# Moving one tile's weighted sum ahead of the next tile's gathers on GpSimd

## The chip, the cores and the metric

One core of one Trainium2 chip. The metric is device microseconds of one execution. Each kernel runs several times; the median is quoted with its lowest and highest run. A separate profiled execution gives the trace, and all times "at" a moment are microseconds from the start of its span.

## The reference, cut to what matters

Input is x of shape (4, 512, 128): four sequences of 512 rows, 2048 rows in all. Four layers follow, each wrapped in a residual and a layer normalisation:

```python
x = _layernorm(x + _L0_attn_ref(x, ...))   # state-space mixer
x = _layernorm(x + _L0_ffn_ref(x, ...))    # mixture of experts: 64 experts, top 8 for each row, and a shared one
x = _layernorm(x + _L1_attn_ref(x, ...))   # attention, 16 heads of 8 columns, bias terms, no mask
x = _layernorm(x + _L1_ffn_ref(x, ...))    # three dense layers with weights of +1 and -1
...
# of the experts' layer:
rw = zeros(T, E).at[rows, topk_idx].add(topk_w)        # 8 weights for each row
routed = jnp.einsum('eth,te->th', expert_out, rw)      # each row's 8 weighted expert rows, summed
out = routed + shared
```

The change concerns the place between the second and the third layer: the weighted sum of each row's 8 expert rows, the normalisation behind it, and the attention that needs it.

## The kernel before, in words

The 2048 rows are 16 tiles of 128 rows (`NT = 16`), four tiles to a sequence (`TB = 4`). Each engine has its own instruction stream, written out by hand, and the streams meet at semaphores.

**Experts.** Rows are scattered to blocks by expert in DRAM (`xd`), pairs of blocks go through the expert's matmuls, and results are written to DRAM (`od`). The first half (tiles 1 to 7) and the second half (tiles 8 to 15) have arrays of their own. For each tile the 8 result rows of each row are then gathered back by 8 indirect DMAs that GpSimd issues (`bring`, L533). For the later tiles GpSimd also forms the sum (`sum_rows`): one multiplication with the weights (L545), three halving additions (L547), one addition of the shared part that writes `tmp` (L548). Each step waits for the one before it, and then `summed` is raised.

**Normalisation.** VectorE waits for `summed`, takes statistics of the four tiles of a sequence (L845, L848) and raises `s_st`. GpSimd makes the reciprocal root from them (`rstd_of`, L469 and L470) and raises `s_rstd`. VectorE then writes the normalised rows (L856), TensorE transposes them (L1516), and ScalarE and TensorE make queries and keys from them.

**Attention.** 16 groups, four for each sequence (`NGR = 16`, `GB = 4`). In group i TensorE does the scores of group i (L1577), their products with the values (L1587) and ahead of time the scores of group i + 2 for the row maxima (L1567). VectorE takes those maxima (L1136), splits them at the end of each group (L1164 to L1173) and normalises the output of the group before (L1150, L1154). ScalarE does the exponentials (L748). The later sequences are prepared inside the groups of the one before: the tables `LATER` and `STATS_IN` set the places. For sequence 2 (tiles 8 to 11) VectorE takes statistics at the end of group 3, and normalisation and transposes stand in group 4. For sequence 3 (tiles 12 to 15) the statistics stand at the end of group 7, the rest in group 8. Sequence 2 is split into parts by VectorE (L1092 to L1098), sequence 3 by GpSimd.

In `dve_group`, the wait that stands between the end of group 3 or 7 and the next group:

```python
if isinstance(i, int) and i + 1 in STATS_IN:
    v.wait_ge(summed, TB * (STATS_IN[i + 1] + 1) - MINE - DENSE)
    stats(tmp, STATS_IN[i + 1])
```

**GpSimd's stream around the change.** While the groups run, GpSimd works through the second half: the 8 gathers of tile t, then the sum of tile t - 1, for t = 9 to 15, and last the sum of tile 15. The root of sequence 2, `rstd_of(2 * B + 2)`, stands behind the first two gathers of tile 13. The root of sequence 3 stands behind the sum of tile 15. Tile t's rows land in a slot of their own (`back_slot`); the slots are four, so tile 12 uses tile 8's slot.

Of the kernel before, what the change touches and what calls it, by code (L numbers as in the profile page):

```python
# [25 lines left out]
TOP_K = 8  # L26
# [5 lines left out]
def build(nc, x, a_log, dmat, w_in, b_in, w_xp, b_xp, w_out, b_out, gamma, beta,  # L32
# [5 lines left out]
    TB = L // P  # L38
# [40 lines left out]
    SLOTS = ((1, 2), (2, 2), (3, 0))  # L79
    STATS_IN = {4: 2, 8: 3}  # L80
    TURN_IN = {i: b for (i, _), (what, b) in LATER.items() if what == "x"}
    PARTS_AT = ((0, 2, 1), (0, 3, 0), (0, 3, 1), (0, 3, 1), (1, 0, 0), (1, 0, 1))
    WRITE_IN = {2: 1, 6: 2, 10: 3}
# [37 lines left out]
    with ExitStack() as ctx:  # L121
# [127 lines left out]
        def back_slot(t):  # L249

            n = t - FIRST[1]
            if n < 0:
                return gb[:, t % 4]
            return late_slot if n % 4 == 3 else gb2[:, n % 4]
# [200 lines left out]
        def _(pool):  # L455
            pn = [0]

            def own(ins):

                pn[0] += 1  # L460
                ins.then_inc(s_p, 1)
                pool.wait_ge(s_p, pn[0])

            def rstd_of(k):

                pool.wait_ge(s_st, k + 1)
                q = k % B
                r = rstd[:, TB * q:TB * q + TB]
                own(pool.tensor_scalar(r, mv[:, TB * q:TB * q + TB, 1], EPS, None, ALU.add))  # L469
                pool.tensor_tensor(r, r, minus_half[:], ALU.pow).then_inc(s_rstd, 1)  # L470
# [57 lines left out]
            def bring(f, t, slot, first=0, last=TOP_K):  # L528

                for k in range(first, last):  # L530
                    if t > DENSE:
                        pool.wait_ge(g_in[k], 16 * (t - DENSE))
                    pool.indirect_dma_start(out=slot[:, k], out_offset=None, in_=od[f],  # L533
                                            in_offset=bass.IndirectOffsetOnAxis(ap=idx[:, t, k:k + 1], axis=0)).then_inc(g_in[k], 16)

            def landed(t):
                for k in range(TOP_K):
                    pool.wait_ge(g_in[k], 16 * (t - DENSE + 1))

            def sum_rows(t):  # L540

                landed(t)
                pool.wait_ge(s_wk, 4 * (t + 1))
                slot = back_slot(t)
                own(pool.tensor_tensor(slot, slot, wk[:, t].unsqueeze(2).broadcast_to([P, TOP_K, M]), ALU.mult))  # L545
                for n in (4, 2, 1):
                    own(pool.tensor_tensor(slot[:, 0:n], slot[:, 0:n], slot[:, n:2 * n], ALU.add))  # L547
                own(pool.tensor_tensor(tmp[:, t], slot[:, 0], xb[:, t], ALU.add))  # L548
                pool.sem_inc(summed, 1)
# [19 lines left out]
            bring(1, FIRST[1], back_slot(FIRST[1]))  # L569
            rstd_of(2 * B + 1)  # L570
            for t in range(FIRST[1] + 1, NT):
                bring(1, t, back_slot(t), 0, 2)
                if t == 3 * TB + 1:
                    rstd_of(2 * B + 2)
                bring(1, t, back_slot(t), 2, TOP_K)
                sum_rows(t - 1)
            sum_rows(NT - 1)

            def qk_parts(b):
# [746 lines left out]
        def _(pe):  # L1326
# [158 lines left out]
            def pe_pairs(first, s0, pairs, beside=None, copied=None, last=None):  # L1485

                ids = {}

                def load_ids(quad, quads=1):

                    _, got = nc.values_load_multi_w_load_instructions(
                        tab[0:1, bass.ds(first + (AHEAD + 4 * quad), 4 * quads)], engines=[mybir.EngineType.PE],
                        min_val=0, max_val=E - 1, skip_runtime_bounds_check_because="the table holds minima with E - 1")
                    for n in range(4 * quads):
                        ids[4 * quad + n] = got[n]

                load_ids(-3, 3)
                for u in range(pairs):
                    later = pairs == 8 and u in (1, 3, 5)
                    pe_pair(s0 + u, u, lambda b: ids[b], (lambda: load_ids(u // 2)) if later else None, beside, copied)  # L1500
                    if last is not None:
                        last(s0 + u)
# [314 lines left out]
```

## Time and profile before

| what | before |
|---|---|
| median of 3 runs | 670.5 us (669.43 to 671.48) |
| the profiled execution: its time, its span | 670.14 us, 668.4 us |
| busy share: TensorE matmul, VectorE, ScalarE, GpSimd | 89%, 72%, 59%, 56% |
| mean granted TensorE clock | 0.953 |
| chain that ended last, by engine | TensorE 57%, VectorE 12%, GpSimd 10%, DMA 7% |
| GpSimd's gathers L533 | 120 of them, about 1 us each |

The busy shares are means over stages with different limits. The row of the chain says which engine's work stood last in line: TensorE most of the time, with stretches of GpSimd in between. The granted clock is 1.00 or 0.50 in any one moment (2.4 or 1.2 GHz); a mean of 0.953 says that it was at the lower level for a few stretches.

### The profile page before, as it was taken

To read this page: it belongs to the slowest core of one execution; us is meant where nothing else is said; L and a number is where in the kernel's file an instruction comes from. 1 tells how busy PE (TensorE), PEld (TensorE's weight loads), DVE (VectorE), ACT (ScalarE), POOL (GpSimd) and SP (SyncE) were. 2 spreads that over 40 slices of the span, in tenths; PEclk is the share of its full clock that TensorE was granted. 3 is DMA by queue.
4 is the path that set the end of the run, shared out by engine and by line. 5 is a ranking of instruction groups with operands and counts; after the bars stand their busy time and mean duration, and the time that the engine had idled before them with its cause. 6 is when DMAs were issued, how large, how long until landed. Compare 5 with 4: busy or idle time off the path is not lost.

```text
span 668.4 us, 13071 instructions
## 1 busy us (share of the span) xinstructions
PE 594.4 (89%) x3696; PEld 371.4 (56%) x3697; DVE 480.3 (72%) x1226; ACT 395.3 (59%) x896; POOL 372.0 (56%) x398
## 2 busy tenths in 40 slices
PE   3973999879999999999886999799989999888994
PEld 2252666659999999999761333233323234344552
DVE  5469743555556656778679788788878886869886
ACT  3411454326666666667657877467777778866541
POOL 6321777777777217775707787887746000235652
PEclk9976799989999999999986999899999999999998
DMA  5999951136777668887454254125203200000001
GB/s 173 434 370 221 399 184 52 52 126 193 225 221 223 197 173 226 224 219 196 131 180 112 70 158 107 42 89 146 53 31 107 71 2 2 1 0 1 17 17 31
DMA packets 98998, 91.51 MB, mean 137 GB/s; under 512 B 10707, under 2 KB 84531, under 8 KB 98739
## 3 DMA queue, kind: packets, MB, share of 16 engines
q1 hardware_dynamic: 91275, 75.24, 37.0%
q0 software_dynamic: 7680, 15.74, 8.3%
q8 instruction: 21, 0.34, 0.2%
q14 instruction: 22, 0.18, 0.1%
HBM read 44.87 MB, written 45.61 MB: 135 GB/s over the span
## 4 chain that ended last, share of the span: by engine, by line
PE 57%; DVE 12%; POOL 10%; DMA 7%; issue 5%; SPq 4%; ACT 3%; POOLq 0%; DVEq 0%; ACTq 0%
PE ps L1472 11%; PE ps L1459 8%; PE ps L1587 6%; PE ps L1577 6%; DMA arena<-zeros 6%; POOL arena L533 4%; PE ps L1567 4%; PE ps L1467 4%; PE ps L1482 4%; PE ps L1384 3%; PE ps L1389 3%; SPq L348 2%; DVE mx L1136 2%; DVE arena L1254 2%; DVE arena L1246 1%
## 5 line engine op out<-in xcount | busy, mean ns | idle before, releaser
L1136 DVE TENSOR_REDUCE mx<-ps 128x2 f32<-128x1024 f32 x128 | 150.9, 1218 | 29.2 <-PE ps L1567 28.6
L748 ACT ACTIVATE big<-ps 128x512 f32<-128x512 f32 x256 | 141.1, 597 | 41.3 <-PE ps L1577 38.6
L521 POOL DMA_INDIRECT xd<-xt,idx x120 | 120.1, 1001 | 49.4 <-issue 35.6
L1472 PE MATMUL ps<-arena,xbT 128*128 x496 | 97.2, 319 | 4.0 <-DVE xbT L1062 4.0
L533 POOL DMA_INDIRECT big<-od,idx x72 | 71.4, 992 | 49.4 <-DMA od<-big 25.0
L1577 PE MATMUL ps<-arena 128*128 128x512 bf16 (+1 forms) x256 | 85.9, 388 | 5.6 <-ACT big L748 4.5
L1058 DVE TENSOR_TENSOR hm<-sg,ps 128x176 f32<-128x176 f32 x124 | 41.8, 337 | 67.0 <-ACT sg L687 65.4
L1567 PE MATMUL ps<-arena 125*128 125x512 bf16 (+1 forms) x256 | 71.8, 394 | 9.2 <-DVE mx L1136 9.0
L1472 PEld LDWEIGHTS ps<-arena,xbT 128*128 128x128 f32 x496 | 76.2, 194 | 4.9 <-issue 4.8
L1459 PE MATMUL ps<-arena,hmT 96*128 x496 | 77.4, 279 | 1.1 <-ACT hmT L683 1.1
L677 ACT ACTIVATE big<-ps 128x256 f32<-128x256 f32 x124 | 47.7, 384 | 47.8 <-PE ps L1459 47.6
L1587 PE MATMUL ps<-big,keep 128*32 128x512 f32 x512 | 69.0, 611 | 0.0
L1577 PEld LDWEIGHTS ps<-arena 128*128 128x128 bf16 (+1 forms) x256 | 20.7, 97 | 86.0 <-ACT big L748 42.9
L1459 PEld LDWEIGHTS ps<-arena,hmT 96*128 96x128 f32 x496 | 65.6, 192 | 3.8 <-issue 1.9
L533 POOL DMA_INDIRECT arena<-od,idx x48 | 46.7, 973 | 32.4 <-DMA od<-big 16.3
L469 POOL TENSOR_SCALAR rstd<-mv 128x4 f32<-128x4 f32 x20 | 5.4, 270 | 102.0 <-DVE mv L848 101.9
L1649 PE MATMUL ps<-arena 128*128 128x512 bf16 x240 | 54.1, 379 | 2.3 <-DVE arena L1246 2.3
L687 ACT ACTIVATE sg<-ps 128x176 f32<-128x176 f32 x124 | 39.4, 318 | 28.0 <-PE ps L1472 23.7
L1062 DVE COPY xbT<-ps 128x256 f32<-128x256 f32 x124 | 51.8, 418 | 0.0
L1467 PE MATMUL ps<-idf,hm 128*96 128x128 f32 x248 | 48.1, 275 | 2.4 <-DVE hm L1058 2.4
L1482 PE MATMUL ps<-idf,big 128*128 128x128 f32 x248 | 48.3, 277 | 0.7 <-DVE xb L912 0.4
L1567 PEld LDWEIGHTS ps<-arena 125*128 125x128 bf16 (+1 forms) x256 | 23.2, 98 | 46.0 <-DVE mx L1136 21.6
(219 smaller groups left out, 994.3 us busy)
## 6 DMA issues: line engine op xcount, KB each, us to landing
big<-xd SPq DMA_DIRECT2D x62, 256.0 KB
od<-big SPq DMA_DIRECT2D x62, 256.0 KB
arena<-scr SPq DMA_DIRECT2D x96, 96.0 KB
xd<-zeros SPq DMA_DIRECT2D x1, 8192.0 KB, 60.5
xd<-zeros SPq DMA_DIRECT2D x1, 7680.0 KB, 21.9
arena<-w_gu SPq DMA_DIRECT2D x1, 5632.0 KB
scr<-places SPq DMA_DIRECT2D x8, 384.0 KB, 2.8
arena<-w_d SPq DMA_DIRECT2D x1, 2560.0 KB
```

The source lines that it names most:

```text
L521: pool.indirect_dma_start(out=xd[f], out_offset=bass.IndirectOffsetOnAxis(ap=idx[:, t, k:k + 1], axis=0), in_=xt[:, t], in_offset=None).th ...
L533: pool.indirect_dma_start(out=slot[:, k], out_offset=None, in_=od[f], in_offset=bass.IndirectOffsetOnAxis(ap=idx[:, t, k:k + 1], axis=0)). ...
L748: act.activation(ering[:, HG * (mt % 2) + h], ps[:, 4 + h % 2, :], ACT.Exp, scale=SCALE).then_inc(exp_ready, 1)
L1136: v.tensor_reduce(mx[:, k, TB * h + 2 * a:TB * h + 2 * a + 2], ps[:, 2 * a:2 * a + 2, :], AX_X, ALU.max).then_inc(s1_free, 1)
L1459: ins = pe.matmul(ps[:, 6 + (u - DN) % 2, M * a:M * a + M], hmT[0:KI, (u - DN) % 2, a], wd_s[0:KI, bass.ds(expert(2 * (u - DN) + a), 1), : ...
L1467: ins = pe.transpose(ps[0:KI, 4 + (u - TH) % 2, P * a:P * a + P], hm[:, (u - TH) % 2, a], idf[:])
L1472: ins = pe.matmul(ps[:, 2 + (u - GU) % 2, I2 * a:I2 * a + I2], xbT[:, (u - GU) % 2, a], wgu_s[:, bass.ds(expert(2 * (u - GU) + a), 1), :]. ...
L1482: ins = pe.transpose(ps[:, u % 2, P * a:P * a + P], xin[:, quad, 2 * part + a], idf[:])
L1567: ins = pe.matmul(ps[:, c, :], flat(kst[0:KM, head(i, h), P * c:P * c + P]), flat(qst[0:KM, head(i, h), :]), start=True, stop=True)
L1577: pe.matmul(ps[:, 4 + h % 2, :], flat(qst[:, head(i, h), P * mt:P * mt + P]), flat(kst[:, head(i, h), :]), start=True, stop=True).then_inc ...
L1587: ins = pe.matmul(ps[32 * h:32 * h + 32, 6, :], vs[:, k, mt, h], ering[:, HG * (mt % 2) + h], start=(mt == 0), stop=(mt == TB - 1))
L1649: ins = pe.matmul(ps[:, n % FC, :], w, h1[b % 2][:, part, kk] if layer else xp[:, part, L * b:L * b + L], start=(kk == 0 and part == 0), s ...
```

## The change

Tile 11's sum now stands in front of tile 12's gathers. The root of sequence 2 stands behind the fourth gather of tile 12, where it stood behind the second gather of tile 13. Elsewhere the order of the loop is as it was.

```diff
             for t in range(FIRST[1] + 1, NT):
-                bring(1, t, back_slot(t), 0, 2)
-                if t == 3 * TB + 1:
+                if t == 3 * TB:
+                    sum_rows(t - 1)
+                bring(1, t, back_slot(t), 0, 4)
+                if t == 3 * TB:
                     rstd_of(2 * B + 2)
-                bring(1, t, back_slot(t), 2, TOP_K)
-                sum_rows(t - 1)
+                bring(1, t, back_slot(t), 4, TOP_K)
+                if t != 3 * TB:
+                    sum_rows(t - 1)
             sum_rows(NT - 1)
```

GpSimd's stream around tile 12, as a difference. The first rows are the end of tile 10's sum; the sum that reads `big` is tile 11's, in whose slot its gathers landed; `rstd` is the root of sequence 2; the `L533` rows are the gathers:

```order
 L547 TENSOR_TENSOR arena<-arena 128x128
 L548 TENSOR_TENSOR tmp<-arena,xb 128x128
-L533 DMA arena<-od,idx 128x128 x8
 L545 TENSOR_TENSOR big<-big,wk 128x1024
 L547 TENSOR_TENSOR big<-big 128x512
```

The eight gathers of tile 12 no longer stand between the sums of tiles 10 and 11. The same stream further on, from the end of tile 11's sum to the beginning of tile 12's:

```order
 L547 TENSOR_TENSOR big<-big 128x128
 L548 TENSOR_TENSOR tmp<-big,xb 128x128
-L533 DMA arena<-od,idx 128x128 x2
+L533 DMA arena<-od,idx 128x128 x4
 L469 TENSOR_SCALAR rstd<-mv 128x4
 L470 TENSOR_TENSOR rstd<-rstd,minus_half 128x4
-L533 DMA arena<-od,idx 128x128 x6
+L533 DMA arena<-od,idx 128x128 x12
 L545 TENSOR_TENSOR arena<-arena,wk 128x1024
```

Four gathers of tile 12 stand ahead of the root, and behind it the other four and the eight of tile 13. The streams of the other engines and of the DMA queue on SyncE have the same instructions in the same order.

## Rows read from the trace of the kernel before

**Rows 1.** The chain of waits: start, length in us, what stood last.
```profile
429.25 1.05 POOL rstd L470
430.34 1.34 DVE xt L856 x4
```

**Rows 2.** Timeline of GpSimd, tiles 11 to 13: start, us, engine, line, operation, idle before.
```profile
404.00 0.94 POOL L533 DMA_INDIRECT big<-od,idx  x1 [0.30 <-issue]
...
409.64 0.45 POOL L548 TENSOR_TENSOR tmp<-arena,xb 128x128 f32<-128x128 f32 x1
410.90 0.98 POOL L533 DMA_INDIRECT arena<-od,idx  x1 [0.81 <-POOL tmp L548]
...
420.65 1.92 POOL L545 TENSOR_TENSOR big<-big,wk 128x1024 f32<-128x1024 f32 x1
...
425.39 0.46 POOL L548 TENSOR_TENSOR tmp<-big,xb 128x128 f32<-128x128 f32 x1
...
429.25 1.04 POOL L470 TENSOR_TENSOR rstd<-rstd,minus_half 128x4 f32<-128x4 f32 x1
430.49 1.16 POOL L533 DMA_INDIRECT arena<-od,idx  x1 [0.19 <-DMA arena<-od,idx]
```

**Rows 3.** Timeline of VectorE, end of group 3 and start of group 4.
```profile
421.56 1.04 DVE L1164 SCALAR_TENSOR_TENSOR mp<-mx,zeros 128x16 bf16<-128x16 f32 x1
...
423.01 0.96 DVE L1170 CAST mp<-mr 128x16 bf16<-128x16 f32 x1
...
425.93 0.87 DVE L845 BATCH_NORM_STATS2 st<-tmp 128x6 f32<-128x128 f32 x4 [1.75 <-POOLq L549]
```

**Rows 4.** Timeline of VectorE, end of group 7.
```profile
482.54 0.17 DVE L1164 SCALAR_TENSOR_TENSOR mp<-mx,zeros 128x16 bf16<-128x16 f32 x1
...
483.42 0.86 DVE L845 BATCH_NORM_STATS2 st<-tmp 128x6 f32<-128x128 f32 x4
```

**Rows 5.** Timeline of GpSimd, tile 15's sum and the root of sequence 3.
```profile
477.55 1.90 POOL L545 TENSOR_TENSOR big<-big,wk 128x1024 f32<-128x1024 f32 x1 [0.53 <-POOL tmp L548]
479.53 2.61 POOL L547 TENSOR_TENSOR big<-big 128x512 f32<-128x512 f32 x3
482.22 0.45 POOL L548 TENSOR_TENSOR tmp<-big,xb 128x128 f32<-128x128 f32 x1
484.79 0.23 POOL L469 TENSOR_SCALAR rstd<-mv 128x4 f32<-128x4 f32 x1 [2.12 <-DVE mv L848]
485.11 1.04 POOL L470 TENSOR_TENSOR rstd<-rstd,minus_half 128x4 f32<-128x4 f32 x1
```

**Rows 6.** Timeline of TensorE's matmuls, start of group 4.
```profile
428.38 0.89 PE L1567 MATMUL ps<-arena 125*128 125x512 bf16 x2 [2.16 <-DVE mx L1136]
...
431.81 1.09 PE L1516 MATMUL ps<-idf,xt 128*128 128x128 f32 x4 [1.27 <-DVE xt L856]
...
435.50 0.60 PE L1577 MATMUL ps<-arena 128*128 128x512 bf16 x2
```

**Rows 7.** The same, start of group 8.
```profile
488.23 0.63 PE L1516 MATMUL ps<-idf,xt 128*128 128x128 f32 x4 [0.63 <-DVE xt L856]
...
490.21 0.69 PE L1577 MATMUL ps<-arena 128*128 128x512 bf16 x2
```

**Rows 8.** Stretches: length, TensorE's busy time, granted clock, DMA share, GB/s.
```profile
357.00:367.00 10.00, 7.14 (x15) 0.50 0.39 107
...
428.00:429.00 1.00, 0.62 (x2) 0.79 0.22 66
429.00:435.00 6.00, 4.49 (x17) 0.50 0.17 44
435.00:436.00 1.00, 1.00 (x7) 0.80 0.10 25
```

**Rows 9.** Timeline of GpSimd: tile 12's halving additions, the second gather of tile 15.
```profile
439.92 3.24 POOL L547 TENSOR_TENSOR arena<-arena 128x512 f32<-128x512 f32 x3
...
463.43 0.95 POOL L533 DMA_INDIRECT big<-od,idx  x1 [2.07 <-issue]
```

## The prediction

> **What bounds the kernel now.** I read the chain of waits first, then the timelines of GpSimd, VectorE and TensorE around the place that the chain names, and last the same stretch one sequence later. The attention groups run at TensorE's pace, and twice the chain leaves TensorE for the stage that prepares the next sequence. The first meeting is at the end of group 3. In the chain there, the root of sequence 2 on GpSimd (L470) releases VectorE's normalisation (L856), which releases TensorE's transposes (L1516) [rows 1]. On GpSimd tile 10's sum ends at 409.64 + 0.45 = 410.09. Tile 12's eight gathers follow from 410.90, though tile 11's last gather was issued at 404.00. Only at 420.65 does tile 11's sum begin, and it ends at 425.39 + 0.46 = 425.85 [rows 2]. VectorE came to the statistics of tiles 8 to 11 earlier: it sat idle 1.75 us before 425.93, so since 424.18, and it would have come sooner still, for L1164 and L1170 took 1.04 and 0.96 us while the sum's long operations ran [rows 3]. At the second meeting, at the end of group 7, VectorE needs tile 15's sum. Its L1164 starts at 482.54 and the statistics at 483.42 with no idle time [rows 4]. GpSimd finished tile 15 at 482.22 + 0.45 = 482.67 [rows 5], 0.75 us before. That is the number on which this prediction turns: GpSimd has 0.75 us to spare there and no more.
>
> **The change at the first meeting.** Nothing is added or removed; eight gathers move behind one sum, and the root behind four gathers of tile 12 instead of two of tile 13.
>
> Tile 11's sum can start at once behind tile 10's. Two sums in a row are 0.53 us apart [rows 5], so it starts at 410.09 + 0.53 = 410.62, runs 425.85 - 420.65 = 5.20, and ends at 415.82 instead of 425.85. Its data are there: the last gather was issued 6.6 us earlier, and a gather's whole pitch is 0.94 + 0.30, about 1.25 us [rows 2].
>
> VectorE at the end of group 3 is then alone. From L1164 to the statistics took 424.18 - 421.56 = 2.62 us [rows 3], and 0.88 at the end of group 7, where no sum ran beside it [rows 4]. So the statistics start at 421.56 + 0.88 = 422.44 instead of 425.93. The root follows as at the second meeting, where L469 starts 1.37 us after the statistics and L470 ends 1.36 us after that [rows 4, 5]: L469 at 423.81, root done 425.17, where it was 430.29.
>
> TensorE's transposes stood at 488.23 in group 8, 4.81 us behind the statistics, and at 431.81 in group 4, 5.88 behind them [rows 6, 7]. So they move to 422.44 + 4.81 = 427.25, a gain of 4.56 us. After them TensorE needed 3.69 us in group 4 to its second pair of L1577 (435.50), but 1.98 in group 8 (490.21) [rows 6, 7], because the granted clock in group 4 was 0.50, the lower of its two levels, after it had sat idle until 428.38 and again before 431.81; in the stretch before 435 it was still 0.50 [rows 8]. With the shorter wait I take group 8's pace, which adds 3.69 - 1.98 = 1.71. **First term: -4.56 - 1.71 = -6.27 us**, and VectorE would reach the second meeting at 483.42 - 6.27 = 477.15.
>
> **The change at the second meeting.** GpSimd does not share this gain, because the same change gives it a wait. Tile 12's gathers start 0.81 us behind the sum as they did before (410.09 to 410.90), so at 415.82 + 0.81 = 416.63. Four of them at the pitch of 1.25 end at about 421.3, with the first a little longer. Then comes the root, and it needs VectorE's statistics, ready for it only at 423.81: GpSimd stands for 2.5 us. Queued behind that wait are four gathers of tile 12, all of tiles 13 to 15, and the sums of 12 to 15, which is everything that the second meeting waits for.
>
> The end of tile 15's sum: before, the root ended at 430.29, and from there to 482.67 GpSimd needed 52.38 us for 6 gathers of tile 13, the 16 of tiles 14 and 15 and four sums. After the root there are now six gathers more (4 of tile 12 and 8 of tile 13, against 6), 6 x 1.25 = 7.5. So 425.17 + 52.38 + 7.5 = 485.05. The statistics of tiles 12 to 15 start at 485.13 with the 0.08 us seen at the first meeting (425.85 to 425.93), instead of 483.42. **Second term: +1.71 us instead of -6.27.** All that groups 4 to 7 gain becomes idle time of VectorE, 477.15 to 485.13, 8 us.
>
> TensorE drains behind it and stands for about as long, longer than at the first meeting before. There the clock fell. So group 8 now pays what group 4 paid, and group 4's saving is already spent. **Third term, the clock: +1.71 us**, by the same pair of rows. Its lower bound is nothing, if the clock is back before the transposes. Its upper bound is from the stretch 357 to 367, where the clock stayed at 0.50 for 10 us with TensorE busy 7.14 of them [rows 8]; half of that work is 3.6 us. I take 1.71, since that stall is the nearest in kind: same engines, same instructions. The Trainium skill (TensorE: Matmul & The Clock Gate, "HAM oscillation — how this bites in real kernels") charges half of the whole time at the lower clock. By that rule the 6.8 us of group 4 (0.4 of the slice from 428, the 6 to 435 and 0.4 of the next) [rows 8] would cost 3.4, and the sum would be +5.1. The trace shows only 1.71 for them, as part of that time was waiting anyway.
>
> Small items. Groups 4 to 7 meet GpSimd's sums at other moments, which may hold VectorE's short operations again; those have 8 us of cover. GpSimd can be held too: tile 12's three L547 took 3.24 us beside VectorE's splitting of sequence 2, against 2.61 for tile 15's [rows 5, 9]. I leave that 0.6 as it is, with 0.6 either way for the range. A gap of 2.07 us stands before a gather of tile 15 [rows 9]; what it waits for is not shown, and it is counted as it stands. The other engines' orders do not change, and from group 9 on everything follows at the same distance.
>
> **Sum:** +1.71 + 1.71 = +3.4 us on a span of 668.4 us, so 671.8, and 670.1 + 3.4 = 673.5 for that execution. Against the median of the runs, 670.5, which stands 0.4 above it, the forecast is **673.9 us**. About 0.3%, or 2.0 us, is what a measurement of this kernel can tell from no change.
>
> **The rivals.**
> - *The low clock lasts long.* A wait of 8 us is longer than any shown at these meetings, and TensorE could stay at the lower level for the 10 us of 357 to 367: 1.71 + 3.6 = +5.3, so 675.8. For it speaks the length of the stall; against it, that TensorE is fully busy soon after the transposes, which it was not there.
> - *The clock costs nothing more.* Only the second term is left, +1.7: 672.2, which is no measurable change. Against it is the fall after a much shorter stall [rows 8].
> - *The gap closes on GpSimd.* If the 2.07 us gap before the gather of tile 15 vanishes with the new timing, tile 15's sum ends at 482.98, and the second term is -0.4. With the clock's 1.7 that is +1.3, 671.8: no measurable change.
> - *The gain stays.* Place: VectorE's wait at the end of group 7. If tile 15's sum were done when VectorE arrives at 477.15, no second stall would come, and the full first term would remain: 664.2. It decides at an end of tile 15's sum of about 481.6, where the second term would just pay the clock (483.42 - 1.71 - 0.08). Some of the gain stays below that. Against it: GpSimd is serial and had no pause near 7 us between 410 and 482; its issue gaps of 0.30 belong to each gather. An unseen faster pitch with fewer holds would have to save over 3.4 us.
> That the change does not do what it says can be set aside: the order shows it, and tile 11's gathers were issued long before.
>
> **How the numbers follow.** Forecast 0.55, long low clock 0.15, no clock cost 0.12, the gap closes 0.12, the gain stays 0.06. Slower by over 0.3%: the forecast and the long clock, 0.70. Within 0.3%: the two in the middle, 0.24. Faster: 0.06. The range leaves out the gain that stays and the ends of the others. It reaches down to the closed gap, 671.8 less 0.6 of contention, 671.2; and up to the long clock plus 0.6 and 0.4 of scatter, 676.8.
>
> **What would show each step.** Tile 11's sum at 410.6 and the root done near 425.2; L1164 and L1170 at the end of group 3 back at 0.2 us; GpSimd idle 2.5 us before L469 behind four gathers; the transposes of group 4 near 427.3 with no fall of the clock there; the sum of tile 15 ending near 485; VectorE idle 7 to 8 us before the statistics of tiles 12 to 15; the clock at 0.50 in group 8 instead of group 4. I am wrong if GpSimd ends tile 15 before 483, if VectorE's wait is not there, or if the clock stays up through it.

## The result and the profile after

| | before | after |
|---|---|---|
| median, runs | 670.36 us, 7 (669.24 to 671.48) | 674.99 us, 7 (672.50 to 676.20) |
| ratio | | 1.0063, 95% interval 1.0046 to 1.0080 |
| profiled execution: time, span | 670.14, 668.4 us | 673.07, 671.3 us |
| mean granted TensorE clock | 0.953 | 0.956 |

The kernel became slower, by 4.2 us as a ratio of 670.36 us. In the two profiled executions the span grew by 2.9 us. The runs after fall into two kinds: three at 672.5, 673.0 and 673.1 us and four from 675.0 to 676.2. The profiled one is of the first kind.

The execution after stood 0.34 us ahead of the one before when the change began (tile 10's sum ends at 409.75 instead of 410.09), so a moment after is compared with the moment before less 0.34. The line numbers from L572 on are higher by 3.

GpSimd's timeline around tiles 11 and 12 (start, us, engine, line, operation, idle before), which answers to [rows 2]:

```profile
410.27 1.90 POOL L545 TENSOR_TENSOR big<-big,wk 128x1024 f32<-128x1024 f32 x1 [0.53 <-POOL tmp L548]
...
414.94 0.45 POOL L548 TENSOR_TENSOR tmp<-big,xb 128x128 f32<-128x128 f32 x1
416.20 0.98 POOL L533 DMA_INDIRECT arena<-od,idx  x1 [0.81 <-POOL tmp L548]
...
419.99 0.94 POOL L533 DMA_INDIRECT arena<-od,idx  x1 [0.30 <-issue]
423.41 0.23 POOL L469 TENSOR_SCALAR rstd<-mv 128x4 f32<-128x4 f32 x1 [2.48 <-DVE mv L851]
423.73 1.04 POOL L470 TENSOR_TENSOR rstd<-rstd,minus_half 128x4 f32<-128x4 f32 x1
```

Tile 11's sum starts at once behind tile 10's. The four gathers follow, and then GpSimd stands for 2.48 us, until VectorE's aggregates (L851) are there. The root ends at 424.77; before it was 430.29.

VectorE at the end of group 3, against [rows 3]:

```profile
421.16 0.17 DVE L1167 SCALAR_TENSOR_TENSOR mp<-mx,zeros 128x16 bf16<-128x16 f32 x1
...
422.04 0.87 DVE L848 BATCH_NORM_STATS2 st<-tmp 128x6 f32<-128x128 f32 x4
```

The short operation takes 0.17 us where it took 1.04, and there is no idle time before the statistics. VectorE's and GpSimd's timelines at the second meeting, against [rows 4, 5]:

```profile
477.30 0.18 DVE L1167 SCALAR_TENSOR_TENSOR mp<-mx,zeros 128x16 bf16<-128x16 f32 x1
...
484.87 0.87 DVE L848 BATCH_NORM_STATS2 st<-tmp 128x6 f32<-128x128 f32 x4 [6.02 <-POOLq L549]
```

```profile
465.50 0.95 POOL L533 DMA_INDIRECT big<-od,idx  x1 [2.07 <-issue]
...
484.33 0.45 POOL L548 TENSOR_TENSOR tmp<-big,xb 128x128 f32<-128x128 f32 x1
486.25 0.23 POOL L469 TENSOR_SCALAR rstd<-mv 128x4 f32<-128x4 f32 x1 [1.46 <-DVE mv L851]
```

VectorE comes early and waits 6.02 us. Tile 15's sum ends at 484.78 instead of 482.67. The pause of 2.07 us before the gather is the same as in [rows 9]. TensorE's matmuls at the start of group 4 and of group 8, against [rows 6, 7]:

```profile
426.85 0.63 PE L1519 MATMUL ps<-idf,xt 128*128 128x128 f32 x4 [0.63 <-DVE xt L859]
...
487.32 2.17 PE L1570 MATMUL ps<-arena 125*128 125x512 bf16 x4 [6.44 <-DVE mx L1139]
489.69 1.09 PE L1519 MATMUL ps<-idf,xt 128*128 128x128 f32 x4 [0.20 <-DVE xt L859]
...
493.25 0.61 PE L1580 MATMUL ps<-arena 128*128 128x512 bf16 x2
```

And TensorE in stretches (length, busy time, granted clock, DMA share, GB/s), against [rows 8]:

```profile
425.00:436.00 11.00, 9.04 (x45) 1.00 0.19 51
486.00:487.00 1.00, 0.00 (x0) 0.60 0.00 0
487.00:493.00 6.00, 5.38 (x18) 0.50 0.01 2
```

Group 4 now runs at the full clock and its transposes start 4.62 us earlier (426.85 against 431.81 - 0.34). Group 8 has what group 4 had before: TensorE stood 6.44 us, the clock fell at 486.2 and was back at 493. From the transposes to the second pair of score matmuls it took 3.56 us there, where [rows 7] had 1.98.

### The profile page after: what moved, and what is told of

It is laid out like the page before. It is cut to its first block, busy times and chain, and to the rows that moved or that the text cites. A ratio compares the mean times of both kernels' runs of the same rounds, so it can differ in the third digit from the quotient of the medians.

```text
span 671.3 us, 13039 instructions
## 1 busy us (share of the span) xinstructions
PE 587.0 (87%) x3664; PEld 369.7 (55%) x3697; DVE 479.7 (71%) x1226; ACT 395.2 (59%) x896; POOL 370.7 (55%) x398
## 4 chain that ended last, share of the span: by engine, by line
PE 56%; DVE 13%; POOL 8%; DMA 7%; issue 6%; ACT 5%; SPq 4%; another core or an unknown queue 1%; POOLq 0%; DVEq 0%; ACTq 0%
PE ps L1475 11%; PE ps L1462 8%; DMA arena<-zeros 6%; PE ps L1580 5%; PE ps L1590 5%; PE ps L1570 4%; PE ps L1470 4%; PE ps L1485 4%; DVE mx L1139 3%; PE ps L1387 3%; PE ps L1392 3%; POOL arena L533 2%; SPq L348 2%; DVE arena L1257 2%; ACT arena L718 2%
## 5 line engine op out<-in xcount | busy, mean ns | idle before, releaser
L533 POOL DMA_INDIRECT big<-od,idx x72 | 71.4, 992 | 53.6 <-DMA od<-big 29.2
L1580 PE MATMUL ps<-arena 128*128 128x512 bf16 (+1 forms) x234 | 79.9, 387 | 7.9 <-ACT big L751 5.0
L1570 PE MATMUL ps<-arena 125*128 125x512 bf16 (+1 forms) x256 | 71.9, 394 | 14.7 <-DVE mx L1139 14.3
L533 POOL DMA_INDIRECT arena<-od,idx x48 | 46.9, 977 | 31.7 <-DMA od<-big 16.1
```

Source lines behind the costliest of these rows:

```text
L1570: ins = pe.matmul(ps[:, c, :], flat(kst[0:KM, head(i, h), P * c:P * c + P]), flat(qst[0:KM, head(i, h), :]), start=True, stop=True)
L1580: pe.matmul(ps[:, 4 + h % 2, :], flat(qst[:, head(i, h), P * mt:P * mt + P]), flat(kst[:, head(i, h), :]), start=True, stop=True).then_inc ...
```

## The experiments

Theory A is that of the prediction: GpSimd is serial, its new wait in front of the root delays everything up to tile 15's sum, and the clock's fall in group 8 comes on top. Theory B is that the moved sum costs by itself. All ratios are against the kernel before, run beside the others on the same chip.

### First measurement: a slower chip, another bound

Four kernels went out together. Three change only the place of the root behind the moved sum. In root_old it stands behind two gathers of tile 13, as before, and the gathers are also split at two instead of four:

```diff
-                if t == 3 * TB:
+                if t == 3 * TB + 1:
                     rstd_of(2 * B + 2)
```

In root_6 six gathers of tile 12 stand ahead of the root instead of four, and in root_0 none (0 for 4 in both lines):

```diff
-                bring(1, t, back_slot(t), 0, 4)
+                bring(1, t, back_slot(t), 0, 6)
...
-                bring(1, t, back_slot(t), 4, TOP_K)
+                bring(1, t, back_slot(t), 6, TOP_K)
```

The fourth, warm, adds matmuls on a constant in front of one score matmul that overwrites their result:

```diff
 def scores(i, mt, h):
...
                 pe.wait_ge(exp_ready, HG * TB * i + (HG * mt + h + 1))
+                if isinstance(i, int) and (i, mt, h) == (2 * GB, 2, 1):
+                    for _ in range(56):
+                        pe.matmul(ps[:, 5, 0:256].rearrange("p (a n) -> p a n", a=2), idb[:],
+                                  idb[:].unsqueeze(1).broadcast_to([P, 2, P]), start=True, stop=True)
```

Expected of root_old:

> Only the sum of tile 11 is moved; the root of sequence 2 stands where it stood before. Theory A (GpSimd's own wait in front of the root is what makes it late at the second meeting): ten gathers stand between the sum and the root, so GpSimd finds the statistics ready and does not wait; the root is done near 430, as before, tile 15's sum ends near 482.7, and the time is that of before, ratio 0.999 to 1.001. Theory B (moving the sum costs by itself, by its data or by holding VectorE): the ratio stays near 1.006.

Expected of root_6:

> The changed kernel with the root behind six gathers of tile 12 instead of four. Theory A: two gathers (2.5 us) fill the wait exactly; the root is done near 425.5, the transposes of group 4 stay near 427, tile 15's sum ends near 482.7, VectorE waits some 4 us there and takes its statistics 0.6 us earlier than before. With the clock's fall (1.7 us) ratio 1.002, without it 0.999. Theory B: ratio near 1.006, as the changed kernel.

Expected of root_0:

> The changed kernel with the root directly behind tile 11's sum, no gather between them. Theory A: GpSimd stands from 415.8 to 423.8, 8 us instead of 2.5, and everything behind it is 5 to 5.5 us later: tile 15's sum ends near 490.4, ratio against before 1.006 + 0.008 = 1.013 to 1.015. Theory B: the time is that of the changed kernel, ratio near 1.006.

Expected of warm:

> The changed kernel; TensorE does 56 more matmuls of 256 columns (about 6 us at full clock), whose result is overwritten, in the middle of its wait at the start of group 8. Theory A with the clock as a term of its own: VectorE's wait stays, the granted clock stays 1.00 in group 8, and the time falls by 1.6 to 1.7 us against the changed kernel, ratio against before about 1.004. Rival C (the slow clock is hidden behind other waits, and the cost above the 1.7 us of lateness has another cause): no change against the changed kernel, ratio near 1.006.

Measured, on a chip on which every kernel took a third longer than in the result:

| | median | ratio, 95% interval |
|---|---|---|
| before | 890.37 us | |
| root_old | 891.97 us | 1.0036 (1.0015 to 1.0058) |
| root_6 | 889.78 us | 1.0005 (0.9986 to 1.0024) |
| root_0 | 891.91 us | 1.0011 (0.9990 to 1.0031) |
| warm | 895.29 us | 1.0077 (1.0049 to 1.0104) |

The list of waits of root_6 (engine, line, waited for: us in total, times, longest) shows where part of the extra time lies:

```profile
PE ps L1392 <- issue: 38.6, 3, 18.9
```

That is 3 pauses of up to 18.9 us in which TensorE waited for nothing that the profile shows; such a row was not among the waits of the kernel before at 670 us. As a test of the two theories by time this measurement does not count. It tells two other things. First, at the second meeting VectorE now comes long after GpSimd. GpSimd's timeline of root_6:

```profile
634.17 0.23 POOL L469 TENSOR_SCALAR rstd<-mv 128x4 f32<-128x4 f32 x1 [12.51 <-DVE mv L851]
634.49 1.05 POOL L470 TENSOR_TENSOR rstd<-rstd,minus_half 128x4 f32<-128x4 f32 x1
...
692.19 0.46 POOL L548 TENSOR_TENSOR tmp<-big,xb 128x128 f32<-128x128 f32 x1
703.90 0.23 POOL L469 TENSOR_SCALAR rstd<-mv 128x4 f32<-128x4 f32 x1 [11.25 <-DVE mv L851]
```

GpSimd stands 12.5 us at the root, and still is done with tile 15 some 10 us before VectorE takes the statistics (702.53). So a wait on GpSimd costs nothing here: root_0, expected at 1.013 to 1.015, has a ratio that can't be told from 1, though GpSimd stood 20.46 us at the root in its profiled execution (900.96 us, the longest of its thirteen). And warm's 56 matmuls had no pause of 6 us to lie in; the ratio of 1.0077 is 6.9 us (the medians differ by 4.9). The ratio of root_old is above 1 by more than its interval, which neither theory expected.

Second, GpSimd's own pace was nearly the same here. From the end of the root to the end of tile 15's sum it took 57.1 us in this profile of root_6 (635.54 to 692.65), with 26 gathers, and 58.2 in the profile of the same kernel at the speed of the result (root_6c, below). At that speed it took 52.4 us with 22 gathers (before) and 60.0 with 28 (after), which is 1.27 us a gather, where the prediction had 1.25.

### Second measurement: the same chip again

> The kernel of root_old again, since all kernels of that call, the one before too, took 890 us, with engines standing still together in stretches of 15 to 20 us that the first trace does not have. Theory A: GpSimd does not wait in front of the root, tile 15's sum ends near 482.7, ratio 0.999 to 1.001. Theory B (moving the sum costs by itself): ratio near 1.006. If the 890 us come back, the call tells nothing on either.

> The kernel of root_6 again, for the same reason. Theory A: the root done near 425.5, tile 15's sum ends near 482.7, VectorE waits some 4 us there; ratio 0.999 without a fall of the clock, 1.002 with it. Theory B: ratio near 1.006, as the changed kernel.

The kernel before took 891.57 us. root_old2 had a ratio of 1.0020 (0.9987 to 1.0052), root_6b 0.9999 (0.9965 to 1.0033). As expected for that case, nothing on either theory.

### The changed kernel again

> The changed kernel itself, once more. If the kernel before takes 670 us here, theory A expects the profile to show again GpSimd idle 2.5 us before the root, VectorE idle 6 to 8 us before the statistics of tiles 12 to 15 and the clock at 0.50 in group 8, ratio 1.004 to 1.008. If it takes 890 us, where in the six profiles so far VectorE reached those statistics 8 to 13 us after tile 15's sum, GpSimd is not the later one at the second meeting, and theory A expects a ratio within 0.998 to 1.002; theory B (the moved instructions cost by themselves) expects the 4 us in either case.

On a chip with the speed of the result: before 671.06 us, the changed kernel 675.13 us, ratio 1.0063 (1.0041 to 1.0085). Its profile has the same three marks: 2.48 us in front of the root, 6.02 us of VectorE before the statistics, and tile 15's sum ending 60.0 us behind the root. The eight runs again leave a gap, three from 672.0 to 672.7 us and five from 674.9 to 678.0.

### Four kernels at the speed of the result

The kernels of root_6, root_old and warm, and one new one. In that, root_6's order of gathers stands, and VectorE forms tile 15's sum itself at the end of group 7 (`sum_last` waits for tile 15's gathers and does the steps of `sum_rows` on VectorE):

```diff
-            sum_rows(NT - 1)
...
-                    v.wait_ge(summed, TB * (STATS_IN[i + 1] + 1) - MINE - DENSE)
-                    stats(tmp, STATS_IN[i + 1])
+                    b = STATS_IN[i + 1]
+                    v.wait_ge(summed, TB * (b + 1) - MINE - DENSE - (b == B - 1))
+                    if b == B - 1:
+                        sum_last(NT - 1)
+                    stats(tmp, b)
```

> The changed kernel with the root behind six gathers of tile 12 instead of four, once more, if the chip gives the 670 us of the kernel before. Theory A: the two gathers fill GpSimd's wait; tile 15's sum ends 2.4 us earlier than in the changed kernel, near 482.6, VectorE's wait shrinks from 6.0 to near 3.6 us and its statistics start near 482.7. With the clock's fall ratio 1.002, without it 0.999. Theory B (moving the sum costs by itself): ratio near 1.006.

> Only the sum of tile 11 moved, the root at its old place, at 670 us. Theory A: no wait of GpSimd in front of the root, root done near 430, tile 15's sum ends near 482.7; VectorE now waits in group 4 for the root, 3 to 4 us, instead of for the sum; ratio 0.999 to 1.001. Theory B: ratio near 1.006.

> The changed kernel with 56 more matmuls inside TensorE's wait at the start of group 8, at 670 us. In the 890 us call they cost 6 us, as there was no wait to hide them. Here theory A with the clock as a term: they lie in the wait of 6.4 us, the granted clock stays 1.00 in group 8, and the time falls by 1.6 us against the changed kernel, ratio 1.003 to 1.004. It also narrows the spread of the changed kernel's runs, if that spread (672.5 and 675.5 us) comes from how long the clock stays low. Rival C (the clock's fall is hidden): ratio stays 1.006.

> Root behind six gathers, and VectorE itself forms tile 15's sum at the end of group 7, in the time in which it would wait. Theory A: GpSimd is done with tile 14 at 477.0 and no longer the last; VectorE arrives near 478.9, needs 2.5 to 3.5 us for the five steps of the sum, and starts its statistics near 482; the pause of TensorE is some 3 us and the clock may stay up: 668 to 669.5 us, ratio 0.996 to 0.999. Theory B: near 1.006.

| | median | ratio, 95% interval |
|---|---|---|
| before | 670.30 us | |
| root_old3 | 670.55 us | 1.0003 (0.9987 to 1.0019) |
| root_6c | 671.71 us | 1.0023 (1.0005 to 1.0041) |
| warm2 | 673.56 us | 1.0043 (1.0026 to 1.0060) |
| root_6_dve15 | 676.72 us | 1.0090 (1.0071 to 1.0108) |

**root_old3** settles A against B as the cause of the loss. The sum is moved as in the changed kernel, and the time is that of the kernel before. GpSimd has no wait in front of the root, VectorE waits for the root in group 4 instead of for the sum:

```profile
429.26 1.33 DVE L859 TENSOR_SCALAR xt<-tmp,mv,rstd 128x128 f32<-128x128 f32 x4 [4.24 <-POOL rstd L470]
```

**root_6c** has the ratio that A expects: two gathers more ahead of the root give back about two thirds of the loss (1.0063 to 1.0023). Its one profile though does not look as I wrote it, so the agreement is one of the number. GpSimd still waits 3.22 us at the root, and VectorE waits only 0.94 at the second meeting (GpSimd, then VectorE):

```profile
426.88 0.23 POOL L469 TENSOR_SCALAR rstd<-mv 128x4 f32<-128x4 f32 x1 [3.22 <-DVE mv L851]
```

```profile
486.53 0.87 DVE L848 BATCH_NORM_STATS2 st<-tmp 128x6 f32<-128x128 f32 x4 [0.94 <-POOLq L549]
```

This execution took 674.5 us, one of the longest of its twelve (669.6 to 675.6). VectorE came late to both meetings. The first lateness is taken up below. The second arose in group 4 (VectorE, then TensorE):

```profile
440.83 2.44 DVE L1101 TENSOR_TENSOR places<-ra,places 128x512 bf16<-128x512 f32 x1
443.19 1.75 DVE L1095 TENSOR_TENSOR ra<-sc,places 128x512 f32<-128x512 f32 x1
```

```profile
446.39 0.29 PE L1600 MATMUL ps<-idb,mp 128*128 128x128 bf16 x1 [3.51 <-DVE mp L1176]
```

These two operations split sequence 2; each took 0.68 us in the profile of the changed kernel (L1101 at 437.36). Here they ran beside tile 12's sum, which began at 440.79. TensorE stood 3.51 us behind them, the clock fell to 0.50 from 446.0 to 449.4, and from the end of group 3 to the end of group 4 it took 20.2 us, against 17.4 in the changed kernel.

The place of the root sets this meeting: tile 12's sum began 12.55 us behind the root's end in root_6c and 15.35 in the changed kernel, while L1101 came 12.6 behind it in both. So every execution with the root behind six gathers should lose this time; that is argued from these rows, since no profile shows a short run of that order.

**warm2** measures the clock. The matmuls lie in the pause, and the fall is gone (TensorE's timeline):

```profile
482.66 6.28 PE L1582 MATMUL ps<-idb 128*128 128x256 bf16 x56 [0.16 <-issue]
...
491.87 0.63 PE L1519 MATMUL ps<-idf,xt 128*128 128x128 f32 x4 [0.63 <-DVE xt L859]
...
493.86 0.70 PE L1584 MATMUL ps<-arena 128*128 128x512 bf16 x2
```

From the transposes to the second pair it takes 1.99 us instead of 3.56: 1.57 us less, where the prediction had 1.71. By the ratios (1.0043 against 1.0063) it is 1.3 us, with overlapping intervals. VectorE waits 6.04 us, as it does in the changed kernel, so this is the clock alone. The spans of the profiled executions say the same. From the end of tile 10's sum to the end it is 258.3 us in the kernel before and in root_old3, 260.0 in warm2, and about 261.6 in both profiles of the changed kernel: 1.7 us for GpSimd's lateness, 1.6 for the clock.

The spread of the runs did not narrow, as I had expected if it came from this stretch: nine runs from 671.3 to 675.3 us.

Half of the whole time at the lower clock, as the Trainium skill charges (TensorE: Matmul & The Clock Gate, "HAM oscillation — how this bites in real kernels"), would be 3.4 us for the 6.8 of group 8; the trace does not agree.

**root_6_dve15** failed: 1.0090 where I expected 0.996 to 0.999. VectorE's timeline:

```profile
485.12 1.23 DVE L1182 TENSOR_TENSOR big<-big,wk 128x1024 f32<-128x1024 f32 x1 [0.22 <-issue]
...
488.21 0.87 DVE L847 BATCH_NORM_STATS2 st<-tmp 128x6 f32<-128x128 f32 x4
```

In this execution VectorE came to the place at 484.9, not 478.9, and GpSimd had ended tile 14 at 479.3. Its splitting in group 4 had been held as in root_6c, L1100 for 2.44 us and L1094 for 1.75. There was no idle time to fill, so the 3.1 us of the sum went onto VectorE's path, and the clock fell as well, from 492.2 to 499. As this fall came late, 6.0 us of it lie behind the transposes, where the changed kernel had 3.3 us, and the way from the transposes to the second pair of projection matmuls (L1537 here, L1525 in the changed kernel, L1522 in the kernel before) took 8.59 us, against 7.34 and 5.85. So 6.8 us at the lower clock cost 2.7 us here and 1.5 there: about half of the part behind the transposes.

The profiled run, of 678.25 us, is the longest of six (675.2 to 678.3). All six are long. The two profiles of this order differ by 4.8 us in the start of the statistics and the price of the clock, and the medians of the two kernels by 5.0, so it fits that in the other runs too VectorE had little idle time left; that is not shown.

### Where the spread of the runs may come from

Seven profiles at this speed can be set side by side. Near 356 us, between the experts and group 0, TensorE waits often and the clock falls. In the profile of the changed kernel and in that of root_6c (stretches, as above):

```profile
356.00:358.00 2.00, 0.85 (x4) 0.62 0.34 72
358.00:366.00 8.00, 5.95 (x12) 0.50 0.43 116
366.00:368.00 2.00, 1.35 (x4) 0.82 0.12 33
```

```profile
356.00:358.00 2.00, 0.85 (x4) 0.80 0.17 43
358.00:370.00 12.00, 9.39 (x20) 0.50 0.35 98
370.00:372.00 2.00, 2.00 (x14) 0.78 0.12 37
```

The lower clock lasts 10.2 us in the one (0.76 of the first two, the 8, and 0.36 of the last two, each share times 2 us) and 13.7 in the other. It is the short stretch in before, both profiles of the changed kernel, root_old3 and warm2, and the long one in root_6c and root_6_dve15. GpSimd does not feel it. From the end of tile 10's sum to VectorE's first splitting operation at the end of group 3 it takes 11.4 to 11.5 us in the five and 14.7 in the two. Of the extra 3.3 us, 1.9 are there at the end of group 2: L1167 came 1.23 us behind the end of tile 10's sum in root_6c and 0.71 before it in the changed kernel. The other 1.4 follow from that, as VectorE's short operations now fall beside the moved sum and are held (VectorE, then GpSimd):

```profile
411.16 1.23 DVE L1167 SCALAR_TENSOR_TENSOR mp<-mx,zeros 128x16 bf16<-128x16 f32 x1
...
412.80 0.96 DVE L1173 CAST mp<-mr 128x16 bf16<-128x16 f32 x1
```

```profile
410.46 1.90 POOL L545 TENSOR_TENSOR big<-big,wk 128x1024 f32<-128x1024 f32 x1 [0.53 <-POOL tmp L548]
412.43 2.66 POOL L547 TENSOR_TENSOR big<-big 128x512 f32<-128x512 f32 x3
```

L1167 ends at 412.39 with GpSimd's L545 at 412.36. In the changed kernel's profile the same operation ran at 409.04, before the sum. The Trainium skill (SBUF — State Buffer, "Who interferes with whom") has the rule: a VectorE instruction with two SBUF inputs contends with a GpSimd instruction that reads SBUF, and what was issued first decides who is held. The trace agrees with it at L1167, which took 1.23 us instead of 0.17 and was issued after L545.

So theory B has a small share where the low clock lasts long. What follows for the runs was argued and then put to a run: in the changed kernel GpSimd waits for VectorE at the root, so 3.3 us more of VectorE's lateness would pass through GpSimd to the second meeting. The gap between the two kinds of its runs is of that size, 2.6 us between their means in the result and 3.7 in the repetition. In the kernel before VectorE is the one that waits at the first meeting, 1.75 us of idling and 1.74 of being held, about 3.5 in all, and that could absorb it.

The spreads speak less clearly: its 7 runs lie within 2.2 us, but its 26 beside the four kernels above within 3.7, as wide as the 3.7 of the changed kernel in the result. Another source is left untested. Tile 10's sum ended between 408.5 and 411.9 us in the seven profiles, though nothing before it differs in the code, and the two profiles of the changed kernel differ by 1.1 us there and by 1.1 us in time.

The run to test the first account keeps TensorE busy there, with matmuls whose result is overwritten:

```diff
 def max_scores(i, h, c):
...
                 if c % 2 == 0:
+                    if isinstance(i, int) and (i == 1 or (i == 0 and h >= 1)):
+                        for _ in range(5):
+                            pe.matmul(ps[:, 5, 0:256].rearrange("p (a n) -> p a n", a=2), idb[:],
+                                      idb[:].unsqueeze(1).broadcast_to([P, 2, P]), start=True, stop=True)
                     pe.wait_ge(s1_free, 2 * HG * i + (2 * h + c // 2 + 1))
```

> The changed kernel with five short matmuls of 256 columns in front of each wait of TensorE for the row maxima of groups 0 and 1 (15 places), so that it is busy there. Theory D: the two kinds of runs of the changed kernel (672.5 and 675.5 us) come from the granted clock after 356 us, which is back at 366 in some and at 369 to 370 in others; the groups then run 3 us later against GpSimd, GpSimd waits 3 us longer in front of the root, and the end moves by that. Without that fall VectorE's statistics are ready when GpSimd comes to the root: it waits 0 to 1 us, tile 15's sum ends 2 us earlier than in the changed kernel, the runs are one group of at most 2.5 us width, ratio 1.000 to 1.003. Rival E (the two kinds come from the stretch after the second meeting): the runs still fall into two groups and the ratio stays at 1.005 or above. If the chip gives 890 us, neither is tested.

It met a chip on which the kernel before took 890.45 us (ratio 1.0011, 0.9988 to 1.0034), and so tested nothing. What the profiles show is that VectorE comes 3.3 us later to the first meeting where the low clock after 356 us lasts long. That this makes the two kinds of runs of the changed kernel is argued: both of its profiles are of the short kind, and both profiles with the long stretch have the root behind six gathers.

## Why the prediction was right

Step by step, as the prediction put it (moments after are raised by 0.34; the end of group 4 is taken at VectorE's first splitting operation, L1164 before and L1167 after):

| step | forecast | measured |
|---|---|---|
| tile 11's sum ends | 415.82 | 415.73 |
| statistics of sequence 2 start | 422.44 | 422.38 |
| GpSimd's wait in front of the root | 2.5 us | 2.48 us |
| root done | 425.17 | 425.11 |
| transposes of group 4 | 427.25 | 427.19 |
| the first term, at the end of group 4 | -6.27 us | 438.56 + 0.34 - 445.15 = -6.25 us |
| VectorE reaches the second meeting | 477.15 | 479.19 |
| tile 15's sum ends | 485.05 | 485.12 |
| term of the second meeting | +1.71 us | 484.87 + 0.34 - 483.42 = +1.79 us |
| clock in group 8 | +1.71 us | +1.58 us (3.56 - 1.98), +1.57 us by warm2 |
| sum, one execution | +3.4 us | +2.9 us of span, +3.3 from the common start |

**The turning number** was the 0.75 us that GpSimd had to spare. It held: the first meeting gave back all it was said to, and none of it reached the end, because GpSimd's wait moved into the chain up to tile 15. root_old3, without that wait, loses nothing.

**VectorE's arrival** was 2.0 us too early in the forecast. Its cover was given as 8 us and was 6.02. The changed order brought a splitting operation of sequence 2 under tile 12's sum: L1099 took 1.70 us where it took 0.42, and TensorE waited 1.47 us for the maxima behind it. The other 0.7 us came at the end of group 7, where L1170 and L1173 took 0.54 and 0.41 us beside tile 14's sum, and 0.12 and 0.16 in the kernel before. The prediction named that risk and its cover, and the cover held.

**The rivals.** The long low clock did not come: 6.8 us in group 8, as in group 4 before. "The clock costs nothing more" is excluded by the profile of warm2; its ratio alone would not do it, as the intervals overlap. The gap before the gather of tile 15 is 2.07 or 2.08 us in every profile. The gain did not stay.

**The size.** The median rose by 4.6 us (4.2 by the ratio) and the forecast was 3.4, which was worked out from one execution. The two profiled executions bear it out, +3.3 us each from the common start, and both are short runs (those of the result are 672.5 to 673.1 us, 2.1 to 2.7 us above the median before). The rest, about 1 us, lies in the long runs. The prediction has no term for them. It had taken one execution's moments for the kernel's, while VectorE's lateness at the first meeting differs by 3.3 us between profiles, and after the change GpSimd waits for it there. That this is the missing 1 us is likely and not shown.

No kernel beat the one before. root_old3 equals it.

## What to carry to other kernels

When two engines meet several times, look at the spare time of each at the next meeting before you relieve the first one: here 6 us won at one meeting were worth nothing, since the other engine had 0.75 us to spare at the next. A small operation that waits for another engine, put early in a serial engine's stream, delays everything behind it; put it behind enough work that its input is ready also in the slower executions, and look at what the work behind it will then run beside. If runs fall into two kinds after a change, ask which wait had absorbed the difference before.

## What the runs showed of the hardware that was not expected

- The time at the lower clock after a stretch with many pauses is not the same in each execution of the same instructions: 10.2 us in five profiles, 13.6 to 13.7 in two, with nothing between. After the single pause in group 8 of the changed kernel it was 6.8. What 6.8 us at the lower clock cost depended on the place: 1.5 to 1.6 us there, 2.7 in group 8 of root_6_dve15.
- The clock fell at different distances behind the last matmul: 5.3 us in group 8 of the changed kernel (480.9 to 486.2), 2.4 us at the first meeting of the kernel before (426.2 to 428.6) and 2.2 us there in root_old3 (425.6 to 427.8). In group 8 of root_6c it fell at 490.3, though TensorE's longest idle times just before were 1.16 and 0.53 us.
- The same program took 670 us in three measurements and 890 us in three others, on two chips, with pauses of TensorE of up to 18.9 us that wait for nothing the profile shows. The order of the kernels in time was not the same there: root_old, equal to the kernel before at 670 us (1.0003), stood at 1.0036 and 1.0020, and root_6, at 1.0023 at 670 us, stood at 1.0005 and 0.9999. The changed kernel itself was not run there.
